# Splitting the score maxima behind their transpose instead of in front of it

## What is computed

```python
x = x + xattn(layernorm(x), ctx_1024)     # x: 16 batches x 112 queries x 256; context: 375 keys
x = x + ffn(layernorm(x))                 # gate from the mean of a batch, then 8 experts, 256 -> 1024 -> 256

def xattn(q, kv):                         # 16 heads of 16 columns
    qp, kp, vp = heads(q @ w_q + b_q), heads(kv @ w_k + b_k), heads(kv @ w_v + b_v)
    attn = softmax(einsum('bhqd,bhkd->bhqk', qp, kp) * SCALE)
    return join(einsum('bhqk,bhkd->bhqd', attn, vp)) @ w_out + b_out
```

## Time and profile before

| | us |
|---|---|
| runs | 969.55, 965.15, 966.83; median 966.83 |
| the profiled execution | 967.49 |
| its span, first to last instruction | 965.4 |
| TensorE busy | 902.7 |
| VectorE busy | 485.9 |
| ScalarE busy | 244.7 |
| GpSimd busy | 236.2 |

### The profile page before, as it was taken

The page is one execution under the profiler, slowest core; times in us unless marked ns, Lnnn a source line. Parts: engine busy times, 40 slices in busy tenths (PEclk is TensorE's granted clock), DMA queues, the critical chain, the costliest instruction groups (busy, mean ns, idle before and its releaser), DMA issues.

```text
span 965.4 us, 17228 instructions
## 1 busy us (share of the span) xinstructions
PE 902.7 (94%) x6250; PEld 746.5 (77%) x6250; DVE 485.9 (50%) x799; ACT 244.7 (25%) x453; POOL 236.2 (24%) x365
## 2 busy tenths in 40 slices
PE   3878898989897899999999999999999999999998
PEld 2757777777775678888888888878888888888887
DVE  6766878787875545555555555543332111212111
ACT  3645666666665310000000000112211001000000
POOL 6444555455533203101001100311103002100000
PEclk9899999999999899999999999999999999999999
DMA  7459666666570181001000100110101001000000
GB/s 186 116 162 230 172 161 166 160 166 161 149 199 14 49 280 52 22 22 34 31 22 22 43 22 22 65 34 33 44 22 66 22 1 44 0 0 0 27 22 27
DMA packets 43798, 74.10 MB, mean 77 GB/s; under 512 B 12378, under 2 KB 33962, under 8 KB 43762
## 3 DMA queue, kind: packets, MB, share of 16 engines
q1 hardware_dynamic: 43762, 73.61, 27.8%
HBM read 56.41 MB, written 17.01 MB: 76 GB/s over the span
## 4 chain that ended last, share of the span: by engine, by line
PE 83%; DVE 9%; DMA 2%; issue 2%; ACT 1%; POOL 1%; SPq 1%; DVEq 0%; ACTq 0%
PE banks L308 41%; PE banks L1511 32%; DVE maxima L969 3%; PE banks L1207 3%; PE banks L1230 2%; PE banks L1248 2%; DVE max_parts L976 2%; PE banks L1493 1%; DMA w_f<-in_wv 1%; DMA k_stack<-k_dram 1%; DVE x_norm L1000 1%; PE banks L1259 1%; ACT xt_parts L777 0%; DVE max_parts L981 0%; PE banks L1287 0%
## 5 line engine op out<-in xcount | busy, mean ns | idle before, releaser
L308 PE MATMUL banks<-w_parts,xt_parts 128*128 128x512 f32 x1344 | 305.9, 389 | 0.0
L308 PEld LDWEIGHTS banks<-w_parts,xt_parts 128*128 128x128 f32 x1344 | 251.9, 188 | 53.8 <-issue 1.1
L1511 PE MATMUL banks<-w_parts,h_high 128*128 (+1 forms) x896 | 240.8, 390 | 1.6 <-DVE h_low L1127 1.6
L1096 DVE SCALAR_TENSOR_TENSOR acc<-banks,gates,acc 128x512 f32<-128x512 f32 x196 | 147.2, 751 | 119.4 <-PE banks L308 119.4
L1511 PEld LDWEIGHTS banks<-w_parts,h_high 128*128 128x128 f32 x896 | 167.2, 188 | 35.9 <-DVE h_low L1127 1.8
L592 POOL TENSOR_TENSOR w_parts<-w_raw,w_parts 128x1024 fp32r<-128x1024 f32 (+1 forms) x32 | 76.4, 2393 | 416.2 <-ACT w_parts L731 416.2
L1121 DVE SCALAR_TENSOR_TENSOR y<-banks,gates,y 128x256 f32<-128x256 f32 x112 | 54.2, 484 | 235.7 <-PE banks L1511 231.4
L1511 PE MATMUL banks<-w_parts,h_low 128*128 (+1 forms) x448 | 138.0, 389 | 0.0
L969 DVE TENSOR_REDUCE maxima<-banks 112x2 f32<-112x750 f32 x128 | 117.6, 934 | 26.4 <-PE banks L1207 23.7
L731 ACT ACTIVATE w_parts<-w_raw 128x1024 fp32r<-128x1024 f32 (+1 forms) x32 | 33.6, 1058 | 354.5 <-PE banks L308 261.1
L694 ACT ACTIVATE probs<-banks 128x448 f32<-128x448 f32 x192 | 100.1, 544 | 20.9 <-PE banks L1230 18.7
(11 more groups left out here) (112 smaller groups left out, 757.6 us busy)
## 6 DMA issues: line engine op xcount, KB each, us to landing
w_raw<-in_w SPq DMA_DIRECT2D x32, 512.0 KB, 3.3
k_dram<-k_parts SPq DMA_DIRECT2D x16, 576.0 KB, 3.1
k_stack<-k_dram SPq DMA_DIRECT2D x32, 288.0 KB, 3.8
k_stack<-k_dram SPq DMA_DIRECT2D x32, 192.0 KB, 4.1
c_raw<-in_ctx_t SPq DMA_DIRECT2D x16, 375.0 KB, 3.8
k_stack<-k_dram SPq DMA_DIRECT2D x32, 96.0 KB, 4.4
b_rows<-gate_dram SPq DMA_DIRECT2D x12, 256.0 KB, 5.0
q_dram<-q_parts SPq DMA_DIRECT2D x16, 168.0 KB, 4.5
```

The source lines that it names most:

```text
L308: last = pe.matmul(out_ap, left(a, k), right(b, k), start=(n == 0), stop=(n == 3 * tiles - 1))
L1096: dve.scalar_tensor_tensor(out=acc[:, t, 512 * s:512 * s + 512], in0=banks[:, t % NB1, :], scalar=gate_col, in1=base[:, 512 * s:512 * s + ...
L1511: last = pe.matmul(banks[:, t % 2, :], h_part[a][:, t, 2 * c + k, :], w, start=(n == 0), stop=(n == 3 * OT - 1))
```

## The change

`max_first` and `max_second` go. The transpose takes the 8 fp32 maxima as they are, with the fp32 identity, and leaves 8 partitions of fp32 in the same PSUM bank. ScalarE copies them out to bf16 (high part, `max_high`), and VectorE subtracts this high part from the PSUM values and writes the rest as bf16 (`max_rest`, counted by `max_low`). `max_rows` is now [8 heads, half, part, 112], and `load_maxima` issues two DMAs, one for each part and row of `q_stack`. Whoever waited for `max_copied` now waits for `max_low`. In VectorE's order `max_rest(s, 1)` stands behind `x_norm`, and `max_rest(nxt, 0)` behind `ot_low`, in front of `reduce_max(nxt, 4)`; in the first step it stands in front of `key_second`. The bf16 identity and its two instructions on GpSimd go, and `max_rows` moves to another place of SBUF.

```diff
@@ -154,14 +154,12 @@
         gates = ffn.take("gates", [P, PAT, C + E], F32)
         keep = Region(ffn.at, nc.sbuf_usable_end)
         ident = keep.take("ident", [P, P], F32)
-        ident_b = keep.take("ident_b", [P, P], BF16)
         ident_e = keep.take("ident_e", [E, E], F32)
         small_sb = keep.take("small_sb", [P, 8 + 2 * E], F32)
         bq_sb, bk_sb, bv_sb, gb1_sb = (small_sb[:, 2 * n:2 * n + 2] for n in range(4))
         gw2_sb = small_sb[:, 8:8 + 2 * E].rearrange("p (k e) -> p k e", k=2)
         gb2_sb = keep.take("gb2_sb", [E, 1], F32)
         gate_t = keep.take("gate_t", [E, P], F32)
-        max_rows = keep.take("max_rows", [D, 2, NQ], BF16)
         stats = keep.take("stats", [NQ, 6], F32)
         mean_var = keep.take("mean_var", [NQ, B, 2], F32)
         half_var = keep.take("half_var", [NQ, B], F32)
@@ -171,7 +169,6 @@
         root_tmp = keep.take("root_tmp", [NQ, B], F32)
         rstd = keep.take("rstd", [NQ, B], F32)
         maxima = keep.take("maxima", [NQ, 2, H], F32)
-        max_parts = keep.take("max_parts", [NQ, 2, 2, HH], BF16)
         recip = keep.take("recip", [NQ, H], F32)
 
 
@@ -186,6 +183,7 @@
         x_norm = front.take("x_norm", [NQ, C], F32)
         x_bias = front.take("x_bias", [NQ, C], F32)
         x_mid = front.take("x_mid", [NQ, 2, C], F32)
+        max_rows = front.take("max_rows", [HH, 2, 2, NQ], BF16)
 
 
         main = Region(at_main, ffn.at)
@@ -238,7 +236,7 @@
 
         banks = psum("banks", [P, 8, 512])
         ps_max = [banks[:, 0:2, :], banks[:, 2:4, :]]
-        ps_max_t = banks[0:D, 2, 384:448].bitcast(BF16)[:, 0:NQ]
+        ps_max_t = banks[0:HH, 2, 384:384 + NQ]
         ps_sc = banks[:, 4:6, :]
         ps_qt = [banks[:, 0:2, :], banks[:, 2:4, :]]
         ps_q = banks[:, 4:6, :]
@@ -272,8 +270,8 @@
         k_stored = sem("k_stored")
         stack_loaded = [[sem(f"stack_loaded{s}{h}") for h in range(2)] for s in range(2)]
 
-        max_mm, max_red, m1_done, m2_done = sem("max_mm"), sem("max_red"), sem("m1_done"), sem("m2_done")
-        max_tr, max_copied = sem("max_tr"), sem("max_copied")
+        max_mm, max_red = sem("max_mm"), sem("max_red")
+        max_tr, max_high, max_low = sem("max_tr"), sem("max_high"), sem("max_low")
         max_loaded = [sem("max_loaded0"), sem("max_loaded1")]
 
         sc_mm, exp_done, pv_mm = sem("sc_mm"), sem("exp_done"), sem("pv_mm")
@@ -381,9 +379,10 @@
                     ).then_inc(stack_loaded[b.slot][h], 16)
 
             def load_maxima(b, h):
-                need(sp, max_copied, b.times(2, h + 1))
-                sp.dma_start(q_stack[QROWS:SROWS, b.slot, h * HH * NQ:(h + 1) * HH * NQ],
-                             max_rows[:, h, :]).then_inc(max_loaded[h], 16)
+                need(sp, max_low, b.times(2, h + 1))
+                for a in range(2):
+                    sp.dma_start(q_stack[QROWS + a:QROWS + a + 1, b.slot, h * HH * NQ:(h + 1) * HH * NQ],
+                                 max_rows[:, h, a, :]).then_inc(max_loaded[h], 16)
 
             def store_keys(b):
 
@@ -471,7 +470,7 @@
 
                     sp.wait_ge(c_low_done, B)
                     sp.wait_ge(v_mm, CH * B)
-                    sp.wait_ge(ident_set, 3)
+                    sp.wait_ge(ident_set, 2)
                     sp.dma_start(eb_sb[:, 0:DFF + C], eb).then_inc(eb_loaded, 16)
                     sp.dma_start(eb_sb[:, DFF + C:GCOLS], ident_e[:]).then_inc(eb_loaded, 16)
                 if s.i is None and s.c == 0:
@@ -536,10 +535,9 @@
         def _(pool):
             pool.memset(c_raw[:, :, :, NKV:KVE], 0.0).then_inc(pad_set, 1)
             pool.memset(ident[:], 0.0).then_inc(zero_set, 1)
-            pool.memset(ident_b[:], 0.0).then_inc(zero_set, 1)
             pool.memset(ident_e[:], 0.0).then_inc(zero_set, 1)
-            pool.wait_ge(zero_set, 3)
-            for m, n in ((ident, P), (ident_b, P), (ident_e, E)):
+            pool.wait_ge(zero_set, 2)
+            for m, n in ((ident, P), (ident_e, E)):
                 pool.affine_select(out=m[:], in_=m[:], compare_op=ALU.not_equal, fill=1.0, base=0,
                                    pattern=[[-1, n]], channel_multiplier=1).then_inc(ident_set, 1)
             pool.memset(magic[:], MAGIC)
@@ -722,8 +720,8 @@
             def max_copy(b, h):
                 if b.exists:
                     need(act, max_tr, b.times(2, h + 1))
-                    need(act, max_loaded[h], b.times(16))
-                    act.activation(max_rows[:, h, :], ps_max_t, ACT.Copy).then_inc(max_copied, 1)
+                    need(act, max_loaded[h], b.times(32))
+                    act.activation(max_rows[:, h, 0, :], ps_max_t, ACT.Copy).then_inc(max_high, 1)
 
             def high_part(loaded, slot, dst):
 
@@ -969,17 +967,11 @@
                     dve.tensor_reduce(maxima[:, b.slot, 2 * k:2 * k + 2], ps_max[k % 2][0:NQ, :, 0:NKV], AX_X, ALU.max)\
                         .then_inc(max_red, 1)
 
-            def max_first(b, h):
+            def max_rest(b, h):
                 if b.exists:
-                    need(dve, max_red, b.times(8, 4 * h + 4))
-                    need(dve, max_tr, b.times(2, h - 1))
-                    dve.tensor_copy(max_parts[:, h, 0, :], maxima[:, b.slot, HH * h:HH * h + HH]).then_inc(m1_done, 1)
-
-            def max_second(b, h):
-                if b.exists:
-                    need(dve, m1_done, b.times(2, h + 1))
-                    dve.tensor_tensor(max_parts[:, h, 1, :], maxima[:, b.slot, HH * h:HH * h + HH],
-                                      max_parts[:, h, 0, :], ALU.subtract).then_inc(m2_done, 1)
+                    need(dve, max_high, b.times(2, h + 1))
+                    dve.tensor_tensor(max_rows[:, h, 1, :], ps_max_t, max_rows[:, h, 0, :], ALU.subtract)\
+                        .then_inc(max_low, 1)
 
             def gate_sum(n):
 
@@ -990,8 +982,6 @@
 
             def step(s):
                 old, last, nxt, new = s + -2, s + -1, s + 1, s + 2
-                max_first(s, 1)
-                max_second(s, 1)
                 if s.i is None and s.c == 0:
                     query_parts(NG - 1)
                 if old.exists:
@@ -999,6 +989,7 @@
                     need(dve, root_done, old.times(ROOT_OPS, ROOT_OPS) + ROOT_OPS * ROOTS)
                     dve.tensor_scalar(x_norm[:], x_mid[:, old.slot, :], mean_var[:, 0, 0:1], rstd[:, 0:1],
                                       ALU.subtract, ALU.mult).then_inc(xn_done, 1)
+                max_rest(s, 1)
                 if nxt.exists_from(1):
                     reduce_max(nxt, 0)
                     reduce_max(nxt, 1)
@@ -1022,14 +1013,15 @@
                     gate_sum(5)
                 reduce_max(nxt, 2)
                 reduce_max(nxt, 3)
-                max_first(nxt, 0)
-                max_second(nxt, 0)
                 if s.i is None and s.c == FIRST_STEP:
+                    max_rest(nxt, 0)
                     key_second(new)
                 if last.exists:
                     need(dve, ot_high_done, last.times(1, 1))
                     dve.tensor_tensor(ot_low[:], ps_w[:, 0:2 * NQ].rearrange("p (a t) -> p a t", a=2), ot_high[:],
                                       ALU.subtract).then_inc(ot_low_done, 1)
+                if not (s.i is None and s.c == FIRST_STEP):
+                    max_rest(nxt, 0)
                 reduce_max(nxt, 4)
                 if last.exists:
 
@@ -1141,7 +1133,7 @@
 
         @block.tensor
         def _(pe):
-            pe.wait_ge(ident_set, 3)
+            pe.wait_ge(ident_set, 2)
             xqt, w_part = (xqt_high, xqt_low), (w_high, w_low)
 
             def query_transpose(g):
@@ -1199,9 +1191,9 @@
                     need(pe, stack_loaded[b.slot][k // 4], b.uses(96))
                 need(pe, max_red, b.times(8, k - 1))
                 if k == 1:
-                    need(pe, max_copied, b.times(2))
+                    need(pe, max_low, b.times(2))
                 if k == 5:
-                    need(pe, max_copied, b.times(2, 1))
+                    need(pe, max_low, b.times(2, 1))
                 for n in range(2):
                     h = 2 * k + n
                     last = pe.matmul(ps_max[k % 2][0:NQ, n, 0:NKV], q_stack[0:QROWS, b.slot, h * NQ:(h + 1) * NQ],
@@ -1211,10 +1203,8 @@
             def max_transpose(b, h):
                 if not b.exists:
                     return
-                need(pe, m2_done, b.times(2, h + 1))
-
                 need(pe, max_red, b.times(8, 8 if h else 4))
-                pe.transpose(ps_max_t, max_parts[:, h].rearrange("p a h -> p (a h)"), ident_b[0:NQ, 0:NQ])\
+                pe.transpose(ps_max_t, maxima[:, b.slot, HH * h:HH * h + HH], ident[0:NQ, 0:NQ])\
                     .then_inc(max_tr, 1)
 
             def scores(b, u):
@@ -1223,7 +1213,7 @@
                     return
                 quarter, c = u // CH, u % CH
                 if u % (2 * CH) == 0:
-                    need(pe, max_loaded[u // (2 * CH)], b.times(16, 16))
```

(1 more changed line is left out.)

## The result

| | before | changed |
|---|---|---|
| median of 12 runs each, us | 968.1 (965.2 to 970.6) | 970.9 (968.3 to 975.3) |
| the profiled execution | 967.49 | 972.88 |
| its span | 965.4 | 971.1 |
| its mean granted clock | 0.988 | 0.979 |

The ratio is 1.0038, interval 1.0021 to 1.0055: 3.7 us slower by the ratio (the two medians differ by 2.8). That is less than the 0.5% set as the bound, but it is a loss that twelve runs can tell from nothing, and the prediction said 963.1, a gain of 3.7. The changed kernel's profiled execution is one of its five slower runs, with a lower clock (see the term on the clock further down), so that more is to be explained in it than in a typical run.

The account below looks back on a forecast made before the run. TensorE was taken as nearly the bound in attention, held up by the maxima transpose's wait for VectorE. Terms -6.3 + 0.5 - 0.2 + 0.7 + 0.9 + 0.7 = -3.7 us gave 963.1, range 956.5 to 971.0.

Parts of the forecast that it names:

- The stall goes (-1.42): TensorE's transpose of the maxima no longer waits for VectorE's held splitting CAST: -1.42 us a step.
- The fp32 transpose (+0.05 each): On TensorE, an fp32 transpose is longer than the bf16 one: +0.05 us each half, +0.10 a step.
- Subtraction 0.27 us, seventh pair +0.21: VectorE's new subtraction takes 0.27 us and delays the fifth reduction, so TensorE's seventh pair of score maxima starts 0.21 later.
- The keys (+0.48): The second maxima DMA on SP delays the key loads queued behind it; TensorE waits 0.48 us a step.
- the rival of a cheap second DMA: On SP, the second DMA issues in 0.42 us or less; a step gives 1.1, in all 957.2; chance 0.24.
- A step, -0.63: One steady attention step, sum of stall, transposes, seventh pair and key wait: -0.63 us; ten intervals -6.3.
- Start-up, -0.2: First batches: +1.2 for the longer DMA pair and later start, 1.4 given back by the stall: -0.2 us.
- later start: Start-up: first subtraction waits for TensorE and ScalarE in front of batch 1's key_second; charged 0.6 us.
- Batch 15, +0.9: Batch 15's key load, on the chain itself, is issued about 0.9 us later behind load_maxima: +0.9.
- Batch 14: Its transpose had no stall to remove, so only the added costs count: +0.7 us.
- x_norm held by GpSimd: In every step GpSimd's k_rest starts first and holds x_norm; a step gives 0.3, in all 966.3; chance 0.14.
- The keys later still: Keys land later than reckoned, TensorE waits 1.1 us, a step gives nothing; 970.3 in all; chance 0.08.

Follow-up runs that it names:

- GpSimd issuing: Changed kernel with both maxima DMAs of half 0 issued by GpSimd instead of SyncE; median 970.6 us, ratio 1.0028 to the kernel before.
- the kernel before with two DMAs: Kernel before with the two score-maxima rows loaded by two DMAs instead of one, nothing else changed; median 976.9 us, ratio 1.0093.
- The orders on VectorE and ScalarE together: Changed kernel with key_second(1) before max_rest(0, 0) on VectorE and max_copy(1, 0) before exp(0, 9) on ScalarE; 969.8 us, ratio 1.0021.
- with that wait filled: Changed kernel with sixteen useless matmuls in TensorE's key wait of batch 2 and ten in batch 15's; 969.5 us, ratio 1.0019.
- key_second first: Changed kernel with key_second(1) in front of max_rest(0, 0) in VectorE's first step; 970.2 us, ratio 1.0027 to the kernel before.

## Why the prediction was wrong, step by step

- **The stall goes (-1.42).** Right; 1.31 with the transpose's own cost in it.
- **The fp32 transpose (+0.05 each).** Mis-sized: 0.11 each, 0.12 us a step.
- **Subtraction 0.27 us, seventh pair +0.21.** Both near (0.26; T+1.83 for T+1.88), but the sum stopped there. The key projection behind the pair came another 0.17 later (T+2.25 for T+1.88). Why is not shown.
- **The keys (+0.48).** The mechanism, the place and the issue time (0.64 us, keys at T+2.46) were right, and the rival of a cheap second DMA is refuted: a step would have gained 0.76 and more, as with GpSimd issuing. The slack was some 0.2 us for the 0.25 that was left in the sum (0.3 less 0.05 for the signal), as the kernel before with two DMAs shows; where TensorE waited for keys in that kernel and in the changed one, it started 0.04 to 0.17 us behind the last landing, 0.1 in the mean. The keys cost 0.52.
- **A step, -0.63.** The measured one is -1.42 + 0.22 + 0.38 + 0.52 = -0.30, and the timelines give -0.33 a step from batch 4 on. The third of a microsecond that is missing is 0.12 for the transposes, 0.17 for the key projection and 0.04 for the keys. Over the ten intervals, the first two of which were bound by late keys from the start-up, the miss is 3.3 us.
- **Start-up, -0.2.** The step that failed most: +3.3. I charged 0.6 us for the "later start" of the subtraction, though its place in the code shows that it waits for a transpose and a copy that ScalarE queues behind an exponential: VectorE waited 2.38 and 2.80 us, and the keys of batches 1 and 2 went out 2.0 and 3.1 us later than before. And I let the stall's 1.4 be given back there, where the keys bind and nothing can be. The orders on VectorE and ScalarE together took it all back (-1.1). The fall of the clock at 83.0 was a small part of it: with that wait filled the start lost 2.7 us instead of 3.3.
- **Batch 15, +0.9.** The wait was 0.77 longer (1.83 for 1.06), as forecast. What was not in the sum is the clock: with the fall behind that wait it was +3.4. Without the fall it was +0.3 in the kernel with key_second first, whose wait was 0.48 longer than before. So the term was large enough for the wait, and what it missed is the clock's. Batch 14 was +1.3 for +0.7.
- **x_norm held by GpSimd.** Did not happen in the steps: 0.41 us at 209.74. **The keys later still** was the rival nearest to the truth (keys used 0.22 later than reckoned), but its losses lay in the steps, and most of the real ones in front of and behind them.
- **The clock as a term.** I had none, though the earlier trace rows show waits for keys at both ends. The changed kernel's twelve runs lie apart with it: seven at 0.984 to 0.986 have a mean of 969.6 us, five at 0.975 to 0.981 one of 973.9. The runs of the kernel before had a median of 0.987 to 0.989 in the four later calls, the changed kernel 0.984. By the slope of its own runs (4.3 us for 0.007) 0.004 are some 2.3 us of the 3.7. That part is worked out from a relation, across calls on several chips, not shown by a run; shown is what a fall costs in one stretch. The profiled execution, at 0.979, is one of the five. Why a fall comes at one wait and not at another (the changed kernel's 1.29 us at 99.10 had none) stays open, and so does which runs get the extra ones.

## What to carry to other kernels

Count a queue in issue times, and measure slack by adding to the queue and looking at the wait that appears; one DMA of 0.64 us cost 0.58 a step in a kernel whose waits showed nothing. When a split of work moves behind another engine's copy, look at the unrolled first steps by themselves: an order that is free in the steady step held the key chain by 2 us there. Before you put a lost microsecond down to a wait, compare the granted clock of both stretches: here two executions with nearly the same wait, 1.83 and 1.54 us, differed by 3.0 us in the same stretch, and the one at half clock was the slower.

## What the runs showed of the hardware

- A DMA of eight short rows between SBUF tensors takes SyncE 634 to 679 ns to issue (641 median, 46 times), a key load out of HBM 322 to 428 in the step shown; a pair issued by GpSimd 1.05 to 1.20 us, landing 3.9 us later in the median (1.5 to 4.7).
- An fp32 transpose of 8 columns is 48 ns longer than a bf16 one of 16 (261 for 213), but TensorE's stream is delayed by 0.11 us.
- Half clock for some 3.4 us in a stretch of 20.4 to 21.2 us made it some 1.5 us longer, for 6.8 us some 3.2 us longer, in fourteen traces.
- In the one trace with ten useless matmuls (1.76 us) in the place of a wait of 1.83 us that stretch was 2.8 us shorter, and the clock stayed at its upper level.
